# A two-layer graph kernel: the order of the first layer's pairs of chunks, and how far the last chunk's chain is spread among them

## Chip, cores and metric

The kernel runs on one core of a Trainium2 chip. The metric is the device time of one execution in microseconds (us), as a median of several runs.

## What is computed

`adj` is a 4096 x 4096 matrix with mostly zeros, `x` has 4096 rows of 128 numbers. First a graph layer in hyperbolic form adds `adj @ v` (with norms, tanh and atanh around two small products) to `x`. Then two attention layers run, each

```
x_norm = x / clip(norm(x), 1e-12)
scores = beta * (x_norm @ x_norm.T)
scores = where(a > 0, scores, -1e9)
x      = leaky(softmax(scores) @ x)
```

on `h = max(layernorm(x), 0)`, and the result is added to `x`. The scores are symmetric: the block of rows A against rows B is the transpose of rows B against rows A. The mask `a` is not symmetric.

## The kernel before

The 4096 rows are NC = 8 chunks of 512. The first stage (to about 282 us) multiplies `adj` by the features, chunk by chunk (`aggregate`), and behind each chunk comes a long chain of small instructions on VectorE and ScalarE that makes the rows of that chunk: lengths, tanh, logarithms, norms, layernorm, and at the end the normalised rows, which TensorE turns into columns `xt`. The chain of the last chunk, 7, is not over when TensorE is, so it is spread over the attention's first steps: `last_chunk(pause)` on ScalarE and VectorE calls `pause(i)` twelve times (PAUSES), and each call, by `between(i)`, is `slot(i + 1)`, one step of the attention.

The attention (`pairs`) works on pairs of chunks (a, b) with b >= a, row by row: a = 0 with b = 0 to 7, then a = 1 with b = 1 to 7, and so on. Each pair is two **halves** (lists at L292 to L308), numbered n from 0 to 143, 72 for each layer. The 16 halves with a = b are diagonal. For a half:

- TensorE makes the scores of 256 columns b against 512 rows a (`pair_scores`, L649).
- ScalarE raises them (`raise_scores`, L1078, one exponential of 128x1024 from PSUM) and makes the high 16 bits (`high_halves`, L1088). VectorE makes the low ones (`low_halves`, L1742).
- VectorE masks them with a tile of `adj` (`own_mask`, L1750), and TensorE adds them times `src` to the sums of row a (`own_sum`, L703 to L707), in the PSUM tile `own_ps`, which gathers a whole row.
- If a < b, TensorE also transposes them (`turns`, L635), VectorE masks the transposed block (`mirrored_mask`, L1760), and TensorE makes the sums for chunk b from it (`mirrored_sum`, L676 to L680) in `mir_ps`. These are added once per pair to `mirror_sums` in SBUF, by `flush` on VectorE (L1769); in row 0 they are the first, so ScalarE copies them (`first_flush`, L1096).

The order is written out by hand as steps n, and each engine has its own program of slots. TensorE in step n: scores of half n, mirrored sum and own sum of half n - 3, column sums if due, transposed columns if due, turns of half n - 1 (L737 to L756). ScalarE in slot n: columns that leave, then a row's first total (row a = 0) or a first flush, exponential n, high halves n, then averages, squares and normalised rows of rows that ended 4, 6 and 9 steps before (L1141). VectorE in slot n: flush of half n - 4, mirrored mask n - 2, a row's total, low halves n - 1, own mask n - 2, then columns, parts of the column sums, leaky (5 steps behind a row's end), the two parts of the scale (7 and 8 steps behind) (L1856). Semaphores join them; every engine works through its list in order.

`turned_at` gives the steps in which rows are turned into columns: chunk 7 of layer 0 at step 12 (LAST_CHUNK_AT), since scores 14 are the first that read it; chunk a of layer 1 ten or eleven steps behind the end of row a. `rows_summed` makes the column sums of `src`, chunk by chunk, in steps 4 to 8, 14 and 15 (SUMS_AT_OF); ScalarE takes them out in slot 16 and VectorE splits them in three parts, which TensorE adds, times a tiny number, to each row's own sum (L714). A row's own sum ends with its last half, is added to `mirror_sums` by `row_total` on VectorE (L1778), for row 0 only copied by ScalarE (`first_total`, L1102); the next row's first own sum waits for that by `total_made` (L694). SyncE loads the tiles of `adj` into six places in the order of the pairs; a load waits for the mask that used the tile six before it.

Of the kernel before, what the change touches and what calls it, by code (L numbers as in the profile page):

```python
# [26 lines left out]
def build(nc, x, adj, adj_t, embed, layer, embed_bias, layer_bias, beta1, beta2, out):  # L27
# [8 lines left out]
    CB = CH // P  # L36
# [30 lines left out]
    with ctx:  # L67
# [224 lines left out]
        Half = namedtuple("Half", "la a b h n off pair row own_tile mir_tile")  # L292
        Row = namedtuple("Row", "la a first last")
        half, rows_of, tile_of = [], [], []
        off_count = [0]
        for la in range(2):
            for a in range(NC):
                rows_of.append(Row(la, a, len(half), len(half) + 2 * (NC - a) - 1))
                for b in range(a, NC):
                    own_tile = len(tile_of)  # L300
                    tile_of.append((b, a, len(half) + 1, None))
                    if b > a:
                        tile_of.append((a, b, len(half) + 1, off_count[0] + 1))
                    for h in range(2):
                        off = off_count[0] if b > a else None
                        off_count[0] += b > a
                        half.append(Half(la, a, b, h, len(half), off, off // 2 if b > a else None, la * NC + a,
                                         own_tile, own_tile + 1))  # L308
# [5 lines left out]
        LAST_CHUNK_AT = 12  # L314
        turned_at = {LAST_CHUNK_AT: (0, NC - 1), **{rows_of[a].last + (11 if a == 5 else 10): (1, a) for a in range(NC)}}
        columns_before = {n: sum(m < n for m in turned_at) for n in turned_at}
        SUMS_AT = 2 * NC - 1
        SUMS_AT_OF = {4: (0, 1), 5: (2,), 6: (3,), 7: (4,), 8: (5,), 14: (6,), SUMS_AT: (7,)}

# [13 lines left out]
        PAUSES = 12  # L333
        ASKS_CHUNK = 6
# [96 lines left out]
        def _(pe):  # L431
# [208 lines left out]
            def pair_scores(x):  # L640

                wait(pe, raised, x.n)
                if x.a == 0 and x.h == 0:
                    pe.wait_ge(xt_lo[x.la], x.b + 1)
# [42 lines left out]
            def own_sum(x):  # L687

                r = rows_of[x.row]
# [3 lines left out]
                if x.n == r.first and x.row != LAST_ROW:  # L693
                    wait(pe, total_made, x.row)  # L694
                own_ps = own_of(x.row)
                if x.n % LAYER == SUMS_AT - 2:
                    pe.wait_ge(sums_copied, x.la + 1)
                w = halves(values[x.n % VR])
                for u in range(HB):
                    for ib in range(CB):  # L700
                        col, q = ds(u * CH + ib * P, P), x.b * CB + x.h * HB + u
                        opens = x.n == r.first and u == 0 and ib % 2 == 0
# [8 lines left out]
                if x.n == r.last:  # L711
# [16 lines left out]
            def columns_turned(n):  # L728
                la, c = turned_at[n]
                rows = rows_n[c % 2] if la else t3  # L730
                pe.wait_ge(xn_ready[la], c + 1)
# [5 lines left out]
            def pairs():  # L737
                for n in range(NH + 4):
# [9 lines left out]
                    if n % LAYER in SUMS_AT_OF and n < NH:  # L748
                        for c in SUMS_AT_OF[n % LAYER]:
                            rows_summed(n // LAYER, c)  # L750
# [20 lines left out]
        def _(act):  # L771
# [319 lines left out]
            def first_flush(x):  # L1091
# [3 lines left out]
                wait(act, total_made, x.la * NC)  # L1095
# [3 lines left out]
            def first_total(i):  # L1099
                act.wait_ge(row_summed, i + 1)  # L1100
# [11 lines left out]
            def row_squares(i):  # L1112
# [6 lines left out]
                nc.scalar.activation(src[1][:, ds(i * CB, CB), F:2 * F], rows_x[i % 2], ACT.Copy, scale=FS)\  # L1119
# [9 lines left out]
            def columns_leave(n):  # L1129
                la, c = turned_at[n]  # L1130
                act.wait_ge(xt_done[la], c + 1)
                if la:
                    wait(act, xt_lo[1], c)
# [7 lines left out]
            def slot(n):  # L1141
                if n % LAYER == SUMS_AT + 1:
                    la = n // LAYER
                    act.wait_ge(sums_done[la], 1)
                    if la:
                        act.wait_ge(row_summed, NC)
# [8 lines left out]
                if i is not None and rows_of[i].a == 0:  # L1155
# [5 lines left out]
                if i is not None and first:  # L1161
# [12 lines left out]
            def between(i):  # L1174

                slot(i + 1)

            def pairs():
                last_chunk(between)
                for n in range(PAUSES + 1, NH + 4):  # L1180
# [12 lines left out]
        def _(dve):  # L1193
# [570 lines left out]
            def flush(x):  # L1764
# [3 lines left out]
                kept = mirror_sums[:, ds(x.b * CB, CB), :].rearrange("p (k b) w -> p k (b w)", k=2)  # L1768
                V.tensor_tensor(kept, kept, mir_ps, ALU.add).then_inc(flushed, 1)  # L1769

            def row_total(i):
# [3 lines left out]
                if r.a:  # L1775
                    dve.wait_ge(row_summed, i + 1)
                    dve.wait_ge(flushed, half[r.first].la * NP + r.a * NC - r.a * (r.a + 1) // 2)
                    V.tensor_tensor(both, last_own_ps if i == LAST_ROW else own_ps, mirror_sums[:, ds(r.a * CB, CB), :]  # L1778
                                    .rearrange("p (k b) w -> p k (b w)", k=2), ALU.add).then_inc(total_made, 1)
                dve.wait_ge(total_made, i + 1)  # L1780
# [51 lines left out]
            def low_rows(i):  # L1832
                q = ds(i * CB, CB)
# [4 lines left out]
            def columns_low(n):  # L1838
                la, c = turned_at[n]
                dve.wait_ge(xt_hi[la], c + 1)  # L1840
# [15 lines left out]
            def slot(n):  # L1856
                x = at(n - 4)
                if x and x.off is not None and x.h == 1 and x.a:
# [5 lines left out]
                if i is not None and rows_of[i].a:  # L1864
# [3 lines left out]
                if i is not None and rows_of[i].a == 0:  # L1868
# [5 lines left out]
                if n % LAYER == SUMS_AT + 1:  # L1874
# [11 lines left out]
            def between(i):  # L1886

                slot(i + 1)

            def pairs():  # L1890
                last_chunk(between)
                for n in range(PAUSES + 1, NH + 1):
# [33 lines left out]
```

## Time and profile before

| | |
|---|---|
| median of 3 runs | 963.98 us (963.15 to 964.41) |
| profiled execution | 963.64 us |
| its span | 962.0 us |
| TensorE busy | 926.9 us, 96% |
| VectorE busy | 792.5 us, 82% |
| ScalarE busy | 538.0 us, 56% |
| granted TensorE clock | 0.997 of full speed |

Busy shares are means over the whole span; the attention begins with scores 0 at 281.7 us. The rows further down show single instructions: for the timelines, start, duration, engine, line, operation, output and inputs, and in brackets the idle time of the engine ahead of it and who ended it.

### The profile page before, as it was taken

What the parts mean: (1) busy time and instruction counts of PE and PEld (TensorE: products, weight loads), DVE (VectorE), ACT (ScalarE), POOL (GpSimd) and SP (SyncE); (2) the same over time, 40 slices, a digit from 0 to 9 for tenths busy, and PEclk for the clock granted to TensorE, in tenths of its full rate; (3) what the DMA queues carried; (4) which work ended last, traced back from release to release, by engine and by line L of the source; (5) the groups of instructions that cost most, each with busy time, mean ns of one, the idle gap of its engine ahead of it and who ended that gap; (6) DMA issues with size and microseconds to landing.
All of it is one profiled execution on the core that took longest, in us unless ns stands there. A gap on an engine that the chain in (4) does not pass through costs nothing.

```text
span 962.0 us, 22931 instructions
## 1 busy us (share of the span) xinstructions
PE 926.9 (96%) x9016; PEld 692.1 (72%) x9016; DVE 792.5 (82%) x1980; ACT 538.0 (56%) x867; POOL 7.2 (1%) x20
## 2 busy tenths in 40 slices
PE   7799999999997999999999999999999999999996
PEld 6644444444445878888888888778888888888886
DVE  7874778777789887978989898998788787888888
ACT  7802222232337766657656667796575565656564
POOL 0000000000000000000000000000000000000000
PEclk9999999999999999999999999999999999999998
DMA  8368888888851555455655545545455555565631
GB/s 298 154 222 289 283 298 293 279 286 283 293 180 57 232 196 210 186 202 198 249 195 212 220 180 216 210 160 201 177 219 219 232 206 201 220 228 194 259 144 37
DMA packets 30419, 207.26 MB, mean 215 GB/s; under 512 B 3632, under 2 KB 4784, under 8 KB 5744
## 3 DMA queue, kind: packets, MB, share of 16 engines
q1 hardware_dynamic: 28752, 203.70, 58.5%
q8 instruction: 71, 1.16, 0.5%
q0 software_dynamic: 560, 1.84, 0.5%
q10 hardware_dynamic: 1008, 0.33, 0.1%
q14 instruction: 28, 0.23, 0.1%
HBM read 203.75 MB, written 2.10 MB: 214 GB/s over the span
## 4 chain that ended last, share of the span: by engine, by line
PE 86%; ACT 6%; DVE 5%; issue 2%; DMA 0%; DVEq 0%; ACTq 0%
PE acc_ps L496 23%; PE s_ps L649 18%; PE s_ps L635 10%; PE acc_ps L707 6%; PE acc_ps L703 6%; PE acc_ps L705 6%; PE acc_ps L680 5%; PE acc_ps L676 5%; PE acc_ps L678 5%; ACT work L1078 1%; ACT set L800 1%; DVE work L1742 1%; PE s_ps L477 1%; ACT xt L822 1%; DVE work L1750 1%
## 5 line engine op out<-in xcount | busy, mean ns | idle before, releaser
L1078 ACT ACTIVATE work<-s_ps,beta_bias,beta_scale 128x1024 f32<-128x1024 f32 x144 | 173.5, 1205 | 212.2 <-PE s_ps L649 212.2
L496 PE MATMUL acc_ps<-ring,set 128*128 128x512 f32 x512 | 222.1, 592 | 1.6 <-DVE set L1348 1.6
L1760 DVE SCALAR_TENSOR_TENSOR h_all<-ring,s_ps 128x1024 f32<-128x1024 f32 x112 | 136.6, 1220 | 65.3 <-PE s_ps L635 63.9
L496 PEld LDWEIGHTS acc_ps<-ring,set 128*128 128x128 f32 x512 | 96.2, 190 | 117.5 <-issue 115.6
L1742 DVE TENSOR_TENSOR work<-work 128x1024 f16<-128x1024 f32 x96 | 132.7, 1382 | 5.4 <-ACT work L1088 5.4
L1088 ACT ACTIVATE work<-work 128x1024 f16<-128x1024 f32 x96 | 131.5, 1370 | 3.0
L1750 DVE SCALAR_TENSOR_TENSOR work<-ring,work 128x1024 f32<-128x1024 f32 x96 | 116.9, 1218 | 0.0
L649 PE MATMUL s_ps<-xt 128*128 128x512 f16 x432 | 105.4, 379 | 4.1 <-ACT work L1078 3.3
L649 PE MATMUL s_ps<-set 128*128 128x512 f16 x432 | 105.0, 379 | 0.5 <-ACT work L1078 0.5
L703 PE MATMUL acc_ps<-src,work 128*128 128x129 f16 x576 | 102.5, 219 | 2.0 <-DVE work L1750 2.0
L707 PE MATMUL acc_ps<-src,work 128*128 128x129 f16 x576 | 102.8, 222 | 0.0
L705 PE MATMUL acc_ps<-src,work 128*128 128x128 f16 x576 | 102.5, 219 | 0.0
L703 PE MATMUL acc_ps<-set,work 128*128 128x129 f16 x560 | 99.6, 219 | 1.2 <-DVE accs L1778 1.2
L707 PE MATMUL acc_ps<-set,work 128*128 128x129 f16 x560 | 99.9, 222 | 0.0
L705 PE MATMUL acc_ps<-set,work 128*128 128x128 f16 x560 | 99.7, 219 | 0.0
L680 PE MATMUL acc_ps<-src,h_all 128*128 128x129 f16 x448 | 79.8, 222 | 0.0
L680 PE MATMUL acc_ps<-set,h_all 128*128 128x129 f16 x448 | 79.8, 222 | 0.0
L676 PE MATMUL acc_ps<-src,h_all 128*128 128x129 f16 x448 | 79.6, 219 | 0.2 <-ACT ring L1096 0.2
L678 PE MATMUL acc_ps<-set,h_all 128*128 128x128 f16 x448 | 79.6, 219 | 0.0
L678 PE MATMUL acc_ps<-src,h_all 128*128 128x128 f16 x448 | 79.6, 219 | 0.0
L676 PE MATMUL acc_ps<-set,h_all 128*128 128x129 f16 x448 | 79.6, 219 | 0.0
L635 PE MATMUL s_ps<-ident,work 128*128 128x128 f32 x560 | 73.7, 275 | 2.3 <-DVE work L1742 2.3
(279 smaller groups left out, 1737.9 us busy)
## 6 DMA issues: line engine op xcount, KB each, us to landing
ring<-in_adj_t SPq DMA_DIRECT2D x192, 1024.0 KB, 5.0
x_sb<-in_x SPq DMA_DIRECT2D x4, 512.0 KB, 7.2
out<-x_sb POOLq DMA_DIRECT2D x7, 256.0 KB, 2.7
out<-x_sb SPq DMA_DIRECT2D x1, 256.0 KB, 2.7
w<-in_layer ACTq DMA_DIRECT2D x2, 64.0 KB, 8.2
w<-in_embed ACTq DMA_DIRECT2D x1, 64.0 KB, 4.5
eb<-in_embed_bias ACTq DMA_DIRECT2D x1, 64.0 KB, 6.9
lb<-in_layer_bias ACTq DMA_DIRECT2D x1, 64.0 KB, 7.9
```

The costliest lines, as they stand in the source:

```text
L496: last = nc.tensor.matmul(agg, v_sb[:, jb, :], ring[:, k, b, :], start=jb == 0, stop=jb == NB - 1)
L635: ins = nc.tensor.transpose(turn_ps[:, ib, ts(u, P)], words[x.n % WR][:, ds(u * CH + ib * P, P)], ident[:, :])
L649: last = nc.tensor.matmul(score_ps[:, ts(u, CH)], xt[x.la][:, p, ds(x.b * CH + (x.h * HB + u) * P, P)], xt[x.la][:, q, ds(x.a * CH, CH)], ...
L676: nc.tensor.matmul(mir_ps[:, x.h, o], w[:, WORD_HI, col], src[x.la][:, q, F:AW], start=ib == 0, stop=False)
L678: nc.tensor.matmul(mir_ps[:, x.h, ds(u * PW, F)], w[:, WORD_HI, col], src[x.la][:, q, 0:F], start=False, stop=False)
L680: last = nc.tensor.matmul(mir_ps[:, x.h, o], w[:, WORD_LO, col], src[x.la][:, q, F:AW], start=False, stop=ib == CB - 1)
L703: nc.tensor.matmul(own_ps[:, ib // 2, ds(ib % 2 * PW, PW)], w[:, WORD_HI, col], src[x.la][:, q, F:AW], start=opens, stop=False, skip_group ...
L705: nc.tensor.matmul(own_ps[:, ib // 2, ds(ib % 2 * PW, F)], w[:, WORD_HI, col], src[x.la][:, q, 0:F], start=False, stop=False, skip_group_c ...
L707: last = nc.tensor.matmul(own_ps[:, ib // 2, ds(ib % 2 * PW, PW)], w[:, WORD_LO, col], src[x.la][:, q, F:AW], start=False, stop=False, ski ...
L1078: nc.scalar.activation(values[x.n % VR], score_ps, ACT.Exp, bias=beta_bias[:, x.la:x.la + 1], scale=beta_scale[:, x.la:x.la + 1]).then_inc ...
L1742: V.tensor_tensor(w[:, WORD_LO, :], values[x.n % VR], w[:, WORD_HI, :], ALU.subtract)\
L1760: V.scalar_tensor_tensor(turned[x.off % MR].rearrange("p (b j) -> p b j", b=CB), ring[:, x.mir_tile % AR, :, ds(x.h * HB * P, HB * P)], 0. ...
```

## The change

In layer 0 the pairs come in another order. Row 0 is b = 0 to 6 (halves 0 to 13). Then comes row 1, b = 1 to 7 (halves 14 to 27). Then the pair of chunks 0 and 7 as a segment of its own, with the roles exchanged: a = 7, b = 0 (halves 28 and 29), so that its own sum belongs to chunk 7 and its mirrored sum to chunk 0. Rows 2 to 7 and layer 1 follow as before.

Chunk 7's columns are first read by scores 26 in place of 14. They are turned at step 24 in place of 12, and each pause of the last chunk's chain is two slots in place of one (SLOTS_PER_PAUSE). The column sums of layer 0 move to steps 18 to 23 and 27.

The own sum of row 0 is copied by ScalarE in slot 17 to `mirror_sums` (`own_kept`). When the late pair is done, VectorE adds to it the mirrored sum out of `mir_ps` and has row 0's total, and adds the late pair's own sum to the sums kept for chunk 7 (`late_total`, slot 33). The products with the parts of the column sums come for row 0 in the late pair's mirrored sum. The first mirrored sum for chunk 7 is now that of pair (1, 7), which VectorE copies instead of adding. Row 1 is over at half 27, row 0 at half 29; the order of chunks in `xn_ready`, `xt_lo` and the totals is counted by the new order.

```diff
+        LATE = NC - 1
+        kept_seg = add_seg(0, 0, range(LATE), None, 0)
+        seg = add_seg(0, 1, range(1, NC), 0, 1)
+        rows_of.append(Row(0, 1, seg.first, seg.last))
+        late_seg = add_seg(0, LATE, (0,), None, 2)
+        rows_of.append(Row(0, 0, kept_seg.first, late_seg.last))
+        LATE_ROW = 1
...
-        LAST_CHUNK_AT = 12
+        LAST_CHUNK_AT = 24
...
-        SUMS_AT_OF = {4: (0, 1), 5: (2,), 6: (3,), 7: (4,), 8: (5,), 14: (6,), SUMS_AT: (7,)}
+        SUMS_AT_LA = (rows_of[0].last, LAYER + 2 * NC - 1)
+        SUMS_AT_OF = {SUMS_AT_LA[0] - 11 + i: c for i, c in {2: (0, 1), 3: (2,), 4: (3,), 5: (4,), 6: (5,), 7: (6,),
+                                                             11: (7,)}.items()}
...
+        SLOTS_PER_PAUSE = 2
...
                         last = nc.tensor.matmul(mir_ps[:, x.h, o], w[:, WORD_LO, col], src[x.la][:, q, F:AW],
-                                                start=False, stop=ib == CB - 1)
+                                                start=False, stop=ib == CB - 1 and x.pair != late_pair)
+                    if x.pair == late_pair:
+                        last = nc.tensor.matmul(mir_ps[:, x.h, o], tiny[:, :], sums_parts, start=False, stop=True)
...
-                if x.n == r.first and x.row != LAST_ROW:
-                    wait(pe, total_made, x.row)
+                if x.n == seg.first and seg.row != LAST_ROW:
+                    wait(pe, total_made, seg.opens_after)
...
+            def own_kept():
+
+                act.wait_ge(own_added, kept_seg.last + 1)
+                nc.scalar.activation(mirror_sums[:, 0:CB, :].rearrange("p (k b) w -> p k (b w)", k=2), own_ps, ACT.Copy)\
+                    .then_inc(total_made, 1)
...
-                if i is not None and rows_of[i].a == 0:
+                own_leaves = n - 4 == kept_seg.last or (i is not None and i == NC)
+                if n - 4 == kept_seg.last:
+                    own_kept()
+                elif i == NC:
                     first_total(i)
...
-                slot(i + 1)
+                for n in range(SLOTS_PER_PAUSE * i + 1, SLOTS_PER_PAUSE * (i + 1) + 1):
+                    slot(n)
...
+                if x.la == 0 and (x.a, x.b) == (1, NC - 1):
+                    V.tensor_copy(kept, mir_ps).then_inc(flushed, 1)
+                    return
+                if x.la == 0 and x.a > 1 and x.b == NC - 1:
+                    dve.wait_ge(total_made, late_seg.opens_after + 1)
                 V.tensor_tensor(kept, kept, mir_ps, ALU.add).then_inc(flushed, 1)
+
+            def late_total():
+
+                late = mirror_sums[:, ds(LATE * CB, CB), :].rearrange("p (k b) w -> p k (b w)", k=2)
+                both, kept = (t.rearrange("p (k b) w -> p k (b w)", k=2) for t in (sums_in, mirror_sums[:, 0:CB, :]))
+                dve.wait_ge(mir_added, half[late_seg.last].off + 1)
+                dve.wait_ge(total_made, 2)
+                dve.wait_ge(flushed, late_pair)
+                V.tensor_tensor(both, kept, mir_ps, ALU.add).then_inc(flushed, 1)
+                dve.wait_ge(own_added, late_seg.last + 1)
+                V.tensor_tensor(late, late, own_ps, ALU.add).then_inc(total_made, 1)
+                dve.wait_ge(flushed, late_pair + 1)
+                V.reciprocal(fin[:, LATE_ROW % 2, 0, :], sums_in[:, :, F]).then_inc(inverse_made, 1)
...
-                if x and x.off is not None and x.h == 1 and x.a:
+                if n - 4 == late_seg.last:
+                    late_total()
+                elif x and x.off is not None and x.h == 1 and x.a:
                     flush(x)
```

The two changed lines of `between` stand alike on ScalarE and VectorE.

## Rows read from the trace of the kernel before

**Rows 1.** The page's share of the chain that ended last, by engine.
```profile
PE 86%; ACT 6%; DVE 5%; issue 2%; DMA 0%; DVEq 0%; ACTq 0%
```

**Rows 2.** Chain of waits, 290 to 480: start us, us, what.
```profile
315.26 1.09 PE s_ps L635 x8
...
396.20 1.29 PE s_ps L649 x6
400.25 0.88 PE s_ps L635 x8
```

**Rows 3.** Timeline of ScalarE, 360 to 412: start us, us, engine line operation [idle before <-releaser].
```profile
361.81 1.21 ACT L1078 ACTIVATE work<-s_ps,beta_bias,beta_scale 128x1024 f32<-128x1024 f32 x1 [2.34 <-PE s_ps L649]
...
367.18 1.21 ACT L1078 ACTIVATE work<-s_ps,beta_bias,beta_scale 128x1024 f32<-128x1024 f32 x1 [1.55 <-PE s_ps L649]
...
390.16 0.29 ACT L1116 ACTIVATE t<-t 128x128 f32<-128x128 f32 x1
...
391.32 0.62 ACT L1119 ACTIVATE set<-t 128x512 f16<-128x512 f32 x1
392.61 1.21 ACT L1078 ACTIVATE work<-s_ps,beta_bias,beta_scale 128x1024 f32<-128x1024 f32 x1 [0.67 <-PE s_ps L649]
```

**Rows 4.** Timeline of ScalarE, 276 to 366.
```profile
301.27 1.21 ACT L1078 ACTIVATE work<-s_ps,beta_bias,beta_scale 128x1024 f32<-128x1024 f32 x1 [3.61 <-PE s_ps L649]
...
306.47 1.21 ACT L1078 ACTIVATE work<-s_ps,beta_bias,beta_scale 128x1024 f32<-128x1024 f32 x1 [2.60 <-PE s_ps L649]
...
309.14 1.28 ACT L786 ACT_TABLE_LOAD   x1
...
325.69 0.28 ACT L910 ACTIVATE t<-t 128x128 f32<-128x128 f32 x1
...
329.10 1.21 ACT L1078 ACTIVATE work<-s_ps,beta_bias,beta_scale 128x1024 f32<-128x1024 f32 x1
```

**Rows 5.** Timeline of VectorE, 378 to 418.
```profile
391.31 1.22 DVE L1760 SCALAR_TENSOR_TENSOR h_all<-ring,s_ps 128x1024 f32<-128x1024 f32 x1 [0.93 <-PE s_ps L635]
392.45 1.38 DVE L1742 TENSOR_TENSOR work<-work 128x1024 f16<-128x1024 f32 x1
...
394.85 0.16 DVE L1820 TENSOR_SCALAR fin<-fin 128x4 f32<-128x4 f32 x1
...
396.04 0.69 DVE L1769 TENSOR_TENSOR ring<-ring,acc_ps 128x516 f32<-128x516 f32 x1
...
400.20 0.15 DVE L1814 TENSOR_TENSOR fin<-fin 128x4 f32<-128x4 f32 x1
...
402.04 1.22 DVE L1760 SCALAR_TENSOR_TENSOR h_all<-ring,s_ps 128x1024 f32<-128x1024 f32 x1
```

**Rows 6.** Timeline of VectorE, 280 to 350.
```profile
296.08 0.17 DVE L1473 COPY small<-small 128x4 f32<-128x4 f32 x1
...
297.50 1.29 DVE L1742 TENSOR_TENSOR h_all<-work,h_all 128x1024 f16<-128x1024 f32 x1
...
310.77 0.16 DVE L1247 TENSOR_TENSOR small<-small 128x4 f32<-128x4 f32 x1 [0.35 <-ACT small L786]
...
312.76 1.22 DVE L1760 SCALAR_TENSOR_TENSOR h_all<-ring,s_ps 128x1024 f32<-128x1024 f32 x1
...
321.75 1.14 DVE L1478 SCALAR_TENSOR_TENSOR t<-t,small,x_sb 128x128 f32<-128x128 f32 x4
...
324.10 1.22 DVE L1760 SCALAR_TENSOR_TENSOR h_all<-ring,s_ps 128x1024 f32<-128x1024 f32 x1
...
334.16 0.17 DVE L1488 TENSOR_SCALAR small<-small 128x4 f32<-128x4 f32 x1 [2.76 <-ACT t L925]
...
335.45 1.22 DVE L1760 SCALAR_TENSOR_TENSOR h_all<-ring,s_ps 128x1024 f32<-128x1024 f32 x1
```

**Rows 7.** Timeline of ScalarE, 600 to 660: marks 73 and 76.
```profile
625.08 1.21 ACT L1078 ACTIVATE work<-s_ps,beta_bias,beta_scale 128x1024 f32<-128x1024 f32 x1 [1.58 <-PE s_ps L649]
...
637.60 1.20 ACT L1078 ACTIVATE work<-s_ps,beta_bias,beta_scale 128x1024 f32<-128x1024 f32 x1
```

More of the change, by code:

```diff
@@ L290, in __call__ @@
                 self.eng.wait_ge(self.s, self.base + self.n)
-        Half = namedtuple("Half", "la a b h n off pair row own_tile mir_tile")
+        Half = namedtuple("Half", "la a b h n off pair seg own_tile mir_tile")
+        Seg = namedtuple("Seg", "first last row opens_after")
         Row = namedtuple("Row", "la a first last")
-        half, rows_of, tile_of = [], [], []
+        half, segs, rows_of, tile_of = [], [], [], []
         off_count = [0]
[L296 to L308, printed above, removed]
@@ new lines, in add_seg @@
+        def add_seg(la, a, bs, row, opens_after):
+            first = len(half)
+            for b in bs:
+                own_tile = len(tile_of)
+                tile_of.append((b, a, len(half) + 1, None))
+                if b != a:
+                    tile_of.append((a, b, len(half) + 1, off_count[0] + 1))
+                for h in range(2):
+                    off = off_count[0] if b != a else None
+                    off_count[0] += b != a
+                    half.append(Half(la, a, b, h, len(half), off, off // 2 if b != a else None, len(segs),
+                                     own_tile, own_tile + 1))
+            segs.append(Seg(first, len(half) - 1, row, opens_after))
+            return segs[-1]
@@ new lines, in build @@
+        LATE = NC - 1
[5 more added lines that the diff above has]
+        LATE_ROW = 1
+        for a in range(2, NC):
+            seg = add_seg(0, a, range(a, NC), a, a + 1)
+            rows_of.append(Row(0, a, seg.first, seg.last))
+        for a in range(NC):
+            seg = add_seg(1, a, range(a, NC), NC + a, NC + 1 + a)
+            rows_of.append(Row(1, a, seg.first, seg.last))
@@ L313, in build, with flushes_before, rows_summed_to, totals_to @@
         row_ending = {r.last: i for i, r in enumerate(rows_of)}
-        LAST_CHUNK_AT = 12
-        turned_at = {LAST_CHUNK_AT: (0, NC - 1), **{rows_of[a].last + (11 if a == 5 else 10): (1, a) for a in range(NC)}}
-        columns_before = {n: sum(m < n for m in turned_at) for n in turned_at}
-        SUMS_AT = 2 * NC - 1
-        SUMS_AT_OF = {4: (0, 1), 5: (2,), 6: (3,), 7: (4,), 8: (5,), 14: (6,), SUMS_AT: (7,)}
+        late_pair = half[late_seg.first].pair
+        def flushes_before(r):
+            return max([x.pair + 1 for x in half if x.off is not None and x.la == r.la and x.b == r.a], default=0)
+        def rows_summed_to(i):
+            return i + 1 - (i >= LATE_ROW)
+        def totals_to(i):
+            return i + 2
+        LAST_CHUNK_AT = 24
+        order_of = {(r.la, r.a): i for i, r in enumerate(rows_of)}
+        turned_at = {LAST_CHUNK_AT: (0, NC - 1), **{r.last + (11 if r.a == 5 else 10): (1, r.a) for r in rows_of[:NC]}}
+        columns_before = {n: sum(m < n for m in turned_at) for n in turned_at}
+        def turn_of(la, c):
+            return order_of[0, c] if la else c
+        SUMS_AT_LA = (rows_of[0].last, LAYER + 2 * NC - 1)
+        SUMS_AT_OF = {SUMS_AT_LA[0] - 11 + i: c for i, c in {2: (0, 1), 3: (2,), 4: (3,), 5: (4,), 6: (5,), 7: (6,),
+                                                             11: (7,)}.items()}
+        SUMS_AT_OF.update({LAYER + i: c for i, c in {4: (0, 1), 5: (2,), 6: (3,), 7: (4,), 8: (5,), 14: (6,),
+                                                     2 * NC - 1: (7,)}.items()})
         def tile_wait(eng, q):
@@ L710, in own_sum @@
                 last.then_inc(own_added, 1)
-                if x.n == r.last:
+                if x.n == seg.last and seg.row is not None:
                     pe.wait_ge(sums_split, 4 * x.la + 4)
@@ L1160, in slot @@
                     raise_scores(at(n))
-                if i is not None and first:
+                if own_leaves and first:
                     first_flush(x)
@@ L1863, in slot @@
                 i = row_ending.get(n - 4)
-                if i is not None and rows_of[i].a:
+                if i is not None and i not in (LATE_ROW, NC):
                     row_total(i)
@@ L1867, in slot @@
                     low_halves(at(n - 1))
-                if i is not None and rows_of[i].a == 0:
+                if i == NC:
                     row_total(i)
@@ L1886, in between @@
             def between(i):
-                slot(i + 1)
+                for n in range(SLOTS_PER_PAUSE * i + 1, SLOTS_PER_PAUSE * (i + 1) + 1):
+                    slot(n)
             def pairs():
                 last_chunk(between)
-                for n in range(PAUSES + 1, NH + 1):
+                for n in range(SLOTS_PER_PAUSE * PAUSES + 1, NH + 1):
                     slot(n)
```

52 lines of the change are left out of this document (27 added, 25 removed).

## Prediction

> **What bounds the kernel now.** I read the chain that ended last first: TensorE is 86% of it [rows 1], so what counts is when TensorE stands still or gets more work. Then I laid the starts of the exponentials (L1078) in a row. The exponential of half n starts when TensorE has finished the scores of half n, so its start is a clock for step n; I call it mark n. A regular step (scores 1.29, mirrored and own sums 400.25 - (396.20 + 1.29) = 2.76, turns 0.88) takes 4.93 us on TensorE alone [rows 2], and the later steps of the trace keep to it. A step whose finished half is diagonal has no mirrored sum (3.55); one whose newest half is diagonal has no turns (4.05). One chunk's column sum (rows_summed) costs 0.44: mark 15 to mark 16 is 5.37 [rows 3]. A transposed column is half of the turns, 0.44.
>
> Now the start. Mark 4 is at 301.27 [rows 4] and mark 15 at 361.81 [rows 3]: 60.54 us. TensorE's own work there is 11 x 4.93 = 54.2, less 1.38 for step 4, plus seven chunks' column sums 3.1, plus one transposed column 0.44: 56.4. So TensorE loses **4.1 us** between these marks, because VectorE and ScalarE carry the last chunk's chain between the slots. This is all that a wider spread can win there.
>
> **How much a slot can carry.** In an undisturbed slot n VectorE begins the mirrored mask 1.30 before mark n (391.31 against mark 22 at 392.61), the low halves end 1.22 after it (392.45 + 1.38), the own mask ends 2.24 after it (394.85) [rows 3, 5]. TensorE wants the low halves at mark + 2.76. So a slot may begin up to 1.5 us late without harm, and a piece of chain behind a slot may last 2.9 us (1.39 idle + 1.5). No piece of pure VectorE work is longer (the longest, chunk_sum, is 2.35: 321.75 to 324.10 [rows 6]). What is too long are the places where VectorE waits for an answer of ScalarE: ScalarE gives it only behind its own slot, at mark + 2.48 and later (the squares of row 0 began at 390.16 [rows 3], mark 21 is 392.61 - 4.93 = 387.68). These places have the same length whether one slot or two precede them. I go through them with the new order; "late" is how much later than usual VectorE begins the next slot.
>
> *Start.* Tanh, column 6's split and chunk_product now stand behind slots 1 and 2. VectorE then no longer has the first part of chunk_norms between the split and low halves 2 (296.08 to 297.50 [rows 6]), but low halves 1 and own mask 0 ahead of chunk_product, and reaches low halves 2 at about 296.5 and not at 297.50. Turns of half 2 go out about 0.95 earlier: mark 4 at 300.3. **Gain 1.0.**
>
> *Behind slot 4: squares (L903).* Four squares with their sums take 391.32 - 390.16 = 1.16 [rows 3]. Mark 4 + 2.48 + 1.16 + handover 0.15: VectorE goes on at mark + 3.8, its piece takes 297.50 - 296.08 = 1.42 [rows 6], slot 5 begins at mark + 5.2, the low halves are there at mark + 7.7, TensorE wanted them at 3.55 + 2.76 = 6.3. **Stop 1.4**, in step 5. Before, it was not waited for here.
>
> *Behind slot 10: logarithms.* With the table load (309.14, 1.28 us) VectorE goes on 4.30 after the mark (310.77 - 306.47) and needs 1.99 more (312.76) [rows 4, 6]. Slot 11 begins at mark + 6.29, low halves at + 8.8, wanted at 4.93 + 2.76 = 7.7. **Stop 1.1**, in step 11. Before, this place stood in a step that held a column sum for cover, and cost little by itself.
> The Trainium skill (ScalarE: Activation LUTs, "What ACT_TABLE_LOAD costs") gives 1283 ns for the load, as the row here, and about 1380 ns of drain on top of it; the row does not show that drain: from the start of the load to VectorE's next instruction, with two logarithms between, are 1.63 us. By the page the stop would be up to 1.4 us longer.
>
> *Behind slot 16: variances (L910, L915), then own_kept.* This is a new wait. Row 0's kept part ends with half 13, and the first own sum of the next segment (half 14, step 17 of TensorE) waits for total_made 1, which own_kept gives at the head of ScalarE's slot 17. Ahead of it in ScalarE's queue stands chunk_variances. Variances and a copy of 128x516 took 329.10 - 325.69 = 3.41 [rows 4]. own_kept is over at mark 16 + 2.48 + 3.41 + 0.05 = 5.9; TensorE is there at 4.05, since step 16 has no turns. Behind the waiting own sum are the turns of half 16 and scores 18. **Stop 1.9**, in step 17.
>
> *Behind slot 18: relu and squares.* VectorE waits here already now: it goes on at 334.16, idle 2.76, which is mark 9 (329.10) + 5.06, and begins the next slot at 335.45, mark + 6.35 [rows 4, 6]. In the new order step 18 has no mirrored sum and the column sums of two chunks (0.9): 4.45. Wanted: 4.45 + 2.76 + 0.45 (the next chunk's column sum) = 7.65; low halves at mark + 8.8. **Stop 1.15**, in step 19.
>
> *After each stop* TensorE is slow for a moment: the turns take 1.09 in place of 0.88 (315.26) [rows 2]. I add 0.2 for each of the four: 0.8.
>
> *Everything else in the chain* fits under the 2.9 us: product_scalars after slot 12, chunk_sum after 14, scales after 20, rows after 22, column 7 at 24. I cost these at nothing; their cover is the 1.39 us of VectorE per slot, and without it each would cost its length. Moved column sums (steps 18 to 23 and 27) keep their number: nothing. The four small products with the sums' parts leave row 0's own sum and come back in the late pair's mirrored sums: nothing. SyncE's tile loads follow the new order of the tiles, each still waits for the mask six tiles back: nothing. GpSimd's memset of layer 1's ones (L409) waits for the last chunk's rows and so goes out some 50 us later; layer 1 reads it 200 us after that: nothing. The copy that takes the place of the flush of pair (1, 7) reads the same 128x516 from PSUM as the add: at most the add's 0.69 [rows 5], at least nothing, and under VectorE's idle time either way.
>
> So the chain's stretch: -1.0 - 4.1 + 1.4 + 1.1 + 1.9 + 1.15 + 0.8 = **+1.2 us**.
>
> **The two row ends.** Row 1 (half 27) and row 0 (half 29) now end two steps apart. Steps 31 to 34 are short (4.05, 4.05, 3.55, 3.55), and into steps 33 to 37 fall two sets of averages, leaky, squares, scales. From the rows: squares with the copy 1.7 on ScalarE (390.16, 391.32 + 0.52), averages about as much as the four squares, 1.2, scale part one 1.19 on VectorE (394.85 to 396.04), part two with low rows 1.84 (400.20 to 402.04) [rows 3, 5], late_total two reads of 128x516 (0.69 each, 396.04) where a flush was one. ScalarE in slot 33 has averages and squares, 2.9: exponential 34 starts 1.8 late and scores 35 wait for it: stop 0.85. VectorE in slots 34 to 36 carries leaky, both parts for row 1, one for row 0; the flush of half 33 comes 0.6 after TensorE wants the bank: stop 0.6, in step 37. With a slow restart 1.6 in all; the two row ends of before lose about 0.3. **+1.3**. The nearest row of before is the end of layer 0, where rows 6 and 7 also end two apart: mark 73 (625.08) to mark 76 (637.60) is 12.5 us [rows 7] for work of 2.68 + 2.91 + 3.55 = 9.1, with four diagonal halves close together, so 3.4 at the worst; 0 is the other bound, if the 2.34 us per slot in which ScalarE is idle (mark 15 [rows 3]) swallow it. I take 1.3, nearer the middle, since here only steps 33 and 34 are that short.
>
> Layers and rows behind step 45 are as before. **Sum: +2.5 us.** The profiled execution took 963.64, 0.34 under the median 963.98. From it 966.1, beside the median **966.5**.
>
> **Rivals.**
> A, *the chain is hidden* (faster). If ScalarE's answers come before VectorE needs them, or the 2.9 us stretch to what the stops need, only the row ends are left: -1.0 - 4.1 + 1.3 = -3.8, **960.2**. For it: pieces of pure VectorE work all fit. Against it: the 2.76 us wait is in the trace and moves along. Chance 0.15.
> B, *stops replace stops* (no change). One or two of my stops, the new own_kept wait or the row ends first, are smaller: -1.9 to +1.9, centre 964.4. For it: each stop is a difference of some 8 us sums. Chance 0.33.
> C, *ScalarE bunches more* (slower still). The row ends cost the 3.4 of layer 0's end, or each load on ScalarE holds it for another load's time (1.28): +3.7 to +5.5, near **968**. Chance 0.08 and 0.02.
> The drain that the Trainium skill states for a table load would belong to this last one.
> D, *the change does not do what it says*: column 7 would still hold scores 26. Against it: rows are ready behind slot 22, at mark 22 + 5.4, while the transposes come at mark 24 + 2.8. Under 0.02, held in B.
> My forecast has 0.42 (its own range 965.9 to 967.6).
>
> **Numbers.** 0.2% is 1.9 us, about what a measurement of this kernel can tell from no change. Slower: 0.42 + 0.10 = 0.52. Within: 0.33. Faster: 0.15. The range from 961.8 to 968.8 leaves out most of A and the end of C.
>
> **What would show it.** Right: mark 4 near 300.3, marks 5 to 6 at 6.5 us, marks 10 to 12 together at 11.2, mark 17 to 18 at 5.4 to 5.5 with TensorE's own sum waiting for a copy of ScalarE, mark 19 to 20 at 6.8, VectorE idle 2.8 before the first instruction of chunk_deviations; marks 33 to 35 at 7.9, mark 37 to 38 at 6.0. From mark 45 on both kernels have the same steps. Wrong: steps 5, 11, 17, 19 at their own work (4.93, 4.93, 3.55, 5.4), which is A; or row ends without a stop, which leaves +1.2 (B).

## The result and the profile after

The changed kernel takes 968.16 us (967.16 to 969.98, 5 runs) beside 963.16 us (962.91 to 964.41, 5 runs) of the kernel before: ratio 1.0046, with a 95% interval of 1.0033 to 1.0058. By the ratio it is slower by 4.4 us (the two medians lie 5.0 apart). Forecast was +2.5, and 966.5 us counted from the median 963.98 of before. The profiled execution took 968.27 us, its span is 966.6.

The page of the changed kernel, its first part and the share of the chain that ended last [rows 1]:

```profile
PE 931.4 (96%) x9016; PEld 695.0 (72%) x9016; DVE 793.7 (82%) x1982; ACT 537.6 (56%) x866; POOL 7.2 (1%) x20
...
PE 86%; ACT 6%; DVE 5%; issue 2%; DMA 0%; DVEq 0%; ACTq 0%
```

The number of matmuls and the shares are the same, so the page's summary does not show where 4.4 us went. The marks do (mark n is the start of the exponential of half n, now L1119; "step n" with a time is the distance from mark n to mark n + 1). I took the starts from ScalarE's timelines of both kernels and of a second profile of each:

| from mark to mark | before | before, again | changed | changed, again | difference | forecast |
|---|---|---|---|---|---|---|
| 0 to 4 | 18.12 | 18.19 | 18.27 | 18.65 | +0.1 to +0.5 | -1.0 |
| 4 to 30 | 131.19 | 131.22 | 132.90 | 132.85 | +1.7 | +1.6 |
| 30 to 45 | 68.64 | 68.64 | 70.88 | 70.95 | +2.3 | +2.0 |
| 45 to 143 | 444.67 | 444.66 | 444.71 | 444.67 | 0.0 | 0 |

(The split of the forecast at mark 30 was made after the result: stops and slow restarts 6.35, less the 4.1 removed, is +2.25 from mark 4 to 30, and 0.67 us of work, a transposed column and four small products of row 0, has moved from there behind mark 30, where it adds to the 1.3 of the row ends.) The stops came as worked out. What failed is the start.

The changed kernel's marks 4, 5 and, further on, 16, 17 and 18, timeline of ScalarE (the kernel before: [rows 3, 4]); L951 is the first of the variances, L1149 is own_kept:

```profile
301.72 1.21 ACT L1119 ACTIVATE work<-s_ps,beta_bias,beta_scale 128x1024 f32<-128x1024 f32 x1 [2.38 <-PE s_ps L688]
...
305.43 1.21 ACT L1119 ACTIVATE work<-s_ps,beta_bias,beta_scale 128x1024 f32<-128x1024 f32 x1
...
361.48 1.21 ACT L1119 ACTIVATE work<-s_ps,beta_bias,beta_scale 128x1024 f32<-128x1024 f32 x1 [1.44 <-PE s_ps L688]
...
363.95 0.28 ACT L951 ACTIVATE t<-t 128x128 f32<-128x128 f32 x1
...
366.79 0.58 ACT L1149 ACTIVATE ring<-acc_ps 128x516 f32<-128x516 f32 x1
367.27 1.19 ACT L1119 ACTIVATE work<-s_ps,beta_bias,beta_scale 128x1024 f32<-128x1024 f32 x1
...
371.26 1.20 ACT L1119 ACTIVATE work<-s_ps,beta_bias,beta_scale 128x1024 f32<-128x1024 f32 x1 [1.07 <-PE s_ps L688]
```

The variances run from 363.95 to 366.79, own_kept at once behind them, with no idle time ahead of either: ScalarE's queue is full just where TensorE needs the copy. Who waited, in the changed kernel between 301 and 400 us (engine and line, what it waited for, us in total, times, longest):

```profile
PE s_ps L672 <- DVE work L1793: 3.4, 3, 1.2
DVE small L1539 <- ACT t L966: 2.8, 1, 2.8
...
PE acc_ps L744 <- ACT ring L1149: 2.0, 1, 2.0
DVE small L1298 <- ACT small L827: 1.9, 1, 1.9
DVE small L1524 <- ACT t L944: 1.4, 1, 1.4
```

There are three waits of VectorE for ScalarE's answers (relu 2.8, logarithms 1.9, squares 1.4), three waits of TensorE for low halves (together 3.4), and one for own_kept (2.0). In the kernel before VectorE did not wait for the squares at all and 0.35 us for the logarithms; the wait for relu is as long as before to the hundredth [rows 6], with two slots ahead of it instead of one:

```profile
376.33 0.17 DVE L1539 TENSOR_SCALAR small<-small 128x4 f32<-128x4 f32 x1 [2.76 <-ACT t L966]
...
377.61 1.22 DVE L1811 SCALAR_TENSOR_TENSOR h_all<-ring,s_ps 128x1024 f32<-128x1024 f32 x1
```

The two row ends, timeline of ScalarE, marks 33, 34, 35, then 37, 38:

```profile
448.10 1.21 ACT L1119 ACTIVATE work<-s_ps,beta_bias,beta_scale 128x1024 f32<-128x1024 f32 x1 [1.55 <-PE s_ps L688]
...
453.43 1.18 ACT L1119 ACTIVATE work<-s_ps,beta_bias,beta_scale 128x1024 f32<-128x1024 f32 x1
...
456.17 1.21 ACT L1119 ACTIVATE work<-s_ps,beta_bias,beta_scale 128x1024 f32<-128x1024 f32 x1 [0.18 <-PE s_ps L688]
...
466.02 1.20 ACT L1119 ACTIVATE work<-s_ps,beta_bias,beta_scale 128x1024 f32<-128x1024 f32 x1 [1.20 <-PE s_ps L688]
...
472.14 1.21 ACT L1119 ACTIVATE work<-s_ps,beta_bias,beta_scale 128x1024 f32<-128x1024 f32 x1 [0.91 <-PE s_ps L688]
```

Exponential 34 has no idle time ahead of it: ScalarE is late. Marks 33 to 35 are 8.07 apart for 7.1 of work, and step 37 takes 6.12 for 5.37 of work.

**The start.** TensorE's timeline of the changed kernel, scores 1, 2, 3, turns 2, scores 4:

```profile
284.71 1.47 PE L688 MATMUL s_ps<-xt 128*128 128x512 f16 x6
...
289.92 2.74 PE L688 MATMUL s_ps<-xt 128*128 128x512 f16 x6 [1.62 <-ACT work L1119]
...
293.96 2.74 PE L688 MATMUL s_ps<-xt 128*128 128x512 f16 x6 [1.30 <-ACT work L1119]
...
299.30 1.09 PE L672 MATMUL s_ps<-ident,h_all 128*128 128x128 f32 x8
300.23 1.46 PE L688 MATMUL s_ps<-xt 128*128 128x512 f16 x6
```

The same six matmuls take 1.47 us and then twice 2.74. The view by stretches of the changed kernel gives the reason (columns: stretch, us, busy time and number for TensorE, its loads, VectorE, ScalarE and GpSimd, then granted clock, DMA share, GB/s):

```profile
283.00:289.50 6.50, 3.84 (x24) 2.36 (x22) 4.99 (x29) 5.92 (x16) 0.00 (x0) 0.96 0.00 0
289.50:299.50 10.00, 8.28 (x38) 4.34 (x39) 8.03 (x17) 7.39 (x8) 0.00 (x0) 0.51 0.01 2
```

and the same of the kernel before:

```profile
283.00:289.50 6.50, 3.53 (x23) 2.17 (x21) 5.02 (x28) 6.22 (x16) 0.00 (x0) 1.00 0.00 0
289.50:299.50 10.00, 5.13 (x42) 3.04 (x43) 9.31 (x24) 8.07 (x16) 0.00 (x0) 1.00 0.01 2
```

TensorE was at 1.2 GHz there (granted clock 0.51), after a stretch in which it had been busy 3.84 of 6.5 us. But both kernels do the same up to 289.6 us, so this profile alone doesn't tell whether the change has a part in it.

### The profile page after: what moved, and what is told of

Its sections match the earlier page's. It is cut to its first block, busy times and chain, and to the rows that moved or that the text cites. A ratio compares the mean times of both kernels' runs of the same rounds, so it can differ in the third digit from the quotient of the medians.

```text
span 966.6 us, 22930 instructions
## 1 busy us (share of the span) xinstructions
PE 931.4 (96%) x9016; PEld 695.0 (72%) x9016; DVE 793.7 (82%) x1982; ACT 537.6 (56%) x866; POOL 7.2 (1%) x20
## 4 chain that ended last, share of the span: by engine, by line
PE 86%; ACT 6%; DVE 5%; issue 2%; DMA 0%; DVEq 0%; ACTq 0%
PE acc_ps L533 23%; PE s_ps L688 18%; PE s_ps L672 10%; PE acc_ps L748 6%; PE acc_ps L744 6%; PE acc_ps L746 6%; PE acc_ps L719 5%; PE acc_ps L715 5%; PE acc_ps L717 5%; ACT work L1119 1%; DVE work L1793 1%; ACT set L841 1%; PE s_ps L514 1%; ACT xt L863 1%; DVE work L1801 1%
## 5 line engine op out<-in xcount | busy, mean ns | idle before, releaser
L1119 ACT ACTIVATE work<-s_ps,beta_bias,beta_scale 128x1024 f32<-128x1024 f32 x144 | 173.4, 1204 | 216.5 <-PE s_ps L688 216.5
L688 PE MATMUL s_ps<-xt 128*128 128x512 f16 x432 | 107.9, 386 | 4.4 <-ACT work L1119 3.6
L744 PE MATMUL acc_ps<-src,work 128*128 128x129 f16 x576 | 103.6, 220 | 2.0 <-ACT ring L1149 2.0
L748 PE MATMUL acc_ps<-src,work 128*128 128x129 f16 x576 | 103.9, 224 | 0.0
```

The lines of the kernel that those rows point to most:

```text
L688: last = nc.tensor.matmul(score_ps[:, ts(u, CH)], xt[x.la][:, p, ds(x.b * CH + (x.h * HB + u) * P, P)], xt[x.la][:, q, ds(x.a * CH, CH)], ...
L744: nc.tensor.matmul(own_ps[:, ib // 2, ds(ib % 2 * PW, PW)], w[:, WORD_HI, col], src[x.la][:, q, F:AW], start=opens, stop=False, skip_group ...
L1119: nc.scalar.activation(values[x.n % VR], score_ps, ACT.Exp, bias=beta_bias[:, x.la:x.la + 1], scale=beta_scale[:, x.la:x.la + 1]).then_inc ...
```

## Experiments

There are three comparisons, each with its own runs of the kernel before, and each ratio is to these: 963.56 us (21 runs) for both kernels again and with ten idle products, 963.91 (26) for the variances, the squares and logarithms, all four answers and row 0's work, 963.45 (21) for the idle products that fit and for everything together. Across comparisons only ratios are compared.

### Both kernels again

No edit.

> The kernel before, unchanged, for the clocks of its executions. In the profile of the changed kernel TensorE stood at half clock from 289.1 to 299.4 us, and scores 2 and 3 took 2.74 us each in place of 1.47. Up to 289.6 both kernels do the same. Theory P (the drop is a matter of phase, not of the change): some executions of this kernel have it too, the mean clock lies between 0.985 and 0.997 and the times spread by 1 to 2 us. Theory Q (the change brings it): all executions at 0.995 to 0.997, scores 2 and 3 at 1.47.

> The changed kernel, unchanged. Theory P: some executions without the drop, at about 966.5 us, and others with it at 967.5 to 968.5. Theory Q: the drop at the same place again, scores 2 and 3 at 2.74 us, mark 4 near 301.7. In both the marks from 5 on have the same distances as in the first profile: 6.4, 4.9 ... and from mark 45 on those of the kernel before.

Before: 963.66 us, ratio 1.0 (0.9991 to 1.0009). Changed: 967.86 us, 1.0053 (1.0040 to 1.0067). In the profile of the kernel before, scores 2 took 2.74 us this time; mark 0 to mark 4 was 18.19, so the half clock cost it nothing (0.07 us):

```profile
289.81 2.74 PE L649 MATMUL s_ps<-xt 128*128 128x512 f16 x6 [1.62 <-ACT work L1078]
...
299.11 1.09 PE L635 MATMUL s_ps<-ident,h_all 128*128 128x128 f32 x8 [1.18 <-DVE h_all L1742]
```

In the changed kernel it came later, at the turns of half 2 and scores 4:

```profile
297.49 1.97 PE L672 MATMUL s_ps<-ident,h_all 128*128 128x128 f32 x8 [2.48 <-DVE h_all L1793]
299.25 2.29 PE L688 MATMUL s_ps<-xt 128*128 128x512 f16 x6
```

Turns 2 went out 14.57 us behind mark 0, as forecast (low halves 2 at 296.5 would put them at 14.7 behind 283.15), and then TensorE lost 1.7 us on turns and scores. In the kernel before they went out 15.77 behind mark 0 (mark 0 is 283.34), and TensorE stood idle ahead of them for 1.18 us, not 2.48.

Theory Q, that the kernel before never has the drop, fell. P stands only in part. The drop at scores 2 comes without the change. The one at turns 2 was in five profiles, all of the changed order and all with 2.5 us of idle time ahead of turns 2, and in neither profile of the kernel before, so the change may well have a part in that one; no run tests it. The mean clock of single executions can't decide it (0.985 to 0.998 in the eleven runs of the kernel before), since profiles have half clock in the kernel's first 45 us as well (0.66 to 0.70 in stretches of 5 us of this one).

### Idle products in the gaps

Ten products (twenty instructions in the trace) whose result nobody reads, in each of three gaps; the edit, the same for both kernels, with WARM_STEPS = 10:

```diff
                     if n == 1:
+                        idle_products(WARM_STEPS)
                         before_last_columns()
+                    if n in (1, 2):
+                        idle_products(WARM_STEPS)
```

> The changed kernel with three lots of ten idle products (128x128, each 0.11 us) for TensorE in the gaps of steps 1 and 2. If the half clock at 289 to 299 costs what I think, it is gone: scores 2 and 3 take 1.47, mark 4 comes at 300.4 to 300.7 and the time falls by 1.0 to 1.4 us beside the changed kernel. If the clock has no part, or the gaps are not what brings it down, time within 0.5 us of the changed kernel.

> The kernel before with the same idle products. Theory P: as fast as the fastest executions of the kernel before, less spread (962.9 to 963.3). Theory Q: no change, 963.2 plus or minus 0.5. If the products themselves delay the scores (they fill only gaps of 1.5 us), up to 0.3 slower.

Changed: 967.53 us, 1.0039 (1.0025 to 1.0053). Before: 963.91, 1.0001 (0.9992 to 1.0010). Both profiles have full clock in the start, but ten products took 2.4 us, not 1.1, longer than the gaps; scores 2 came 1.0 us late, and mark 0 to 4 in the changed kernel was 17.98, not 17.2. That is inconclusive for the cost, so I cut the products to fit (the edit against the kernels without idle products):

```diff
+                    if n == 3:
+                        idle_products(8)
                     if done:
                         own_sum(done)
...
                     if n == 1:
+                        idle_products(5)
                         before_last_columns()
+                    if n in (1, 2):
+                        idle_products(5)
```

> The changed kernel with idle products that fit TensorE's gaps: five (1.2 us) in each of the three gaps of steps 1 and 2, eight ahead of own sum 0 (the ten of before took 2.4 us and pushed scores 2 by 1.2). Theory (the start gains 1.0 us only if TensorE is at full clock between 289 and 301): no half clock there, mark 4 at mark 0 + 17.2 to 17.4 in place of 18.27 and 18.65, and 1.0 to 1.4 us off the time. Rival (something else holds the start): mark 0 to mark 4 at 18 or more with the clock full.

> The kernel before with the same idle products. Its scores 2 and 3 have slack: VectorE's chain orders the start, so a half clock there cost it nothing (mark 0 to 4 was 18.12 at full clock and 18.19 with 3.4 us at half). Theory: mark 0 to 4 stays at 18.1 to 18.2, time within 0.4 us. Rival (the clock costs both kernels the same): 0.5 us or more less.

TensorE's timeline of the changed kernel with them (L473 are the idle products):

```profile
288.33 1.28 PE L473 MATMUL acc_ps<-ident 128*128 128x128 f32 x10
290.13 1.47 PE L688 MATMUL s_ps<-xt 128*128 128x512 f16 x6 [0.52 <-ACT work L1124]
291.44 1.28 PE L473 MATMUL acc_ps<-ident 128*128 128x128 f32 x10
292.90 1.47 PE L688 MATMUL s_ps<-xt 128*128 128x512 f16 x6 [0.19 <-ACT work L1124]
```

Mark 0 to 4 is 17.02 at full clock: the start's gain of 1.0 us is there once the clock holds (the forecast's marks gave 17.15). In the kernel before it is 18.11, no gain: there VectorE's chain orders the start, and turns 2 go out 15.7 us behind mark 0 at full clock as at half. The time of the changed kernel did not follow: 967.70 us, 1.0042 (1.0029 to 1.0056), where 1.0 to 1.4 less was expected. Its profile has half clock at another stop, that of step 17:

```profile
366.50:370.50 4.00, 3.94 (x33) 3.90 (x34) 0.00 (x0) 2.75 (x3) 0.00 (x0) 0.58 0.81 266
```

Marks 16 to 18 took 11.41 us there, in place of 9.78. But the profiled execution was the slowest of the five (968.68). The other four took 967.19 to 967.79 at a higher mean clock (0.995, not 0.992), and 968.68 less 1.63 is 967.05, so this stop explains the profiled execution and not the median. For the changed kernel the gain of the start is thus shown in the marks of one profile and not in the time; why the time did not follow is open. Before: 963.77 us, 1.0004 (0.9995 to 1.0013).

Over all profiles of this study, the granted clock between 289 and 302 us was 0.61 to 0.88 in eight of the nine without idle products (only the first profile of the kernel before had 1.00), and 1.00 in all five with them.

### Variances one slot earlier

ScalarE calls them behind slot 15 and not 16 (`slots(a, b)` calls slots a to b; `pause(i)` was slots 2i + 1 and 2i + 2):

```diff
-                for i in (6, 7):
-                    pause(i)
+                slots(13, 15)
                 chunk_variances()
-                pause(8)
+                slots(16, 18)
```

> The changed kernel; ScalarE makes the variances of the last chunk behind slot 15 in place of slot 16, so that own_kept no longer stands behind them. Theory (ScalarE's queue makes the stop in step 17): TensorE's 2.0 us of waiting for that copy is gone, marks 16 to 18 are 7.6 to 7.8 us apart in place of 9.78, and the time falls by about 2.0 us beside the changed kernel. Rival (the place is one where all engines are full, so the stop comes back behind it): marks 16 to 18 shorter, marks 18 to 20 longer by the same, time within 0.5.

966.23 us, 1.0026 (1.0016 to 1.0036): 1.9 to 2.6 us less than the changed kernel, by its ratios of 1.0046 and 1.0053. Timeline of ScalarE, marks 16 to 18 with own_kept (L1151):

```profile
362.61 1.18 ACT L1121 ACTIVATE work<-s_ps,beta_bias,beta_scale 128x1024 f32<-128x1024 f32 x1
...
365.04 0.57 ACT L1151 ACTIVATE ring<-acc_ps 128x516 f32<-128x516 f32 x1
365.51 1.19 ACT L1121 ACTIVATE work<-s_ps,beta_bias,beta_scale 128x1024 f32<-128x1024 f32 x1
...
369.50 1.20 ACT L1121 ACTIVATE work<-s_ps,beta_bias,beta_scale 128x1024 f32<-128x1024 f32 x1 [1.06 <-PE s_ps L688]
```

Marks 16 to 18 are 6.89 apart in place of 9.78, but exponential 16 starts 1.3 late behind the variances; marks 15 to 18, which hold both, went from 13.81 to 12.22. So 1.6 us are won in the marks (expected were 2.0), and steps 18 and 19 are unchanged (5.45, 5.80): nothing came back behind it. ScalarE's queue made this stop.

### Squares and logarithms one slot earlier

```diff
-                pause(1)
+                slots(3, 3)
                 chunk_squares()
-                for i in (2, 3, 4):
-                    pause(i)
+                slots(4, 9)
                 log_terms(sm(4, CB), sm(5, CB), sm(6, CB))
```

> The changed kernel; ScalarE makes the squares behind slot 3 in place of 4 and the logarithms behind slot 9 in place of 10. Theory (VectorE waits for an answer that comes too late in ScalarE's slot): VectorE no longer idles there (1.43 and 1.9 us now), step 5 falls from 6.37 to 4.93 to 5.2, marks 10 to 12 from 11.17 to 9.9, together 2.7 us less. Rival (the length of VectorE's own piece makes the stops): steps unchanged, time within 0.5.

966.34 us, 1.0020 (1.0011 to 1.0030), in ten runs from 964.52 to 967.22. Timeline of ScalarE, marks 5 and 6, then the two table loads and mark 10 behind them:

```profile
305.87 1.21 ACT L1121 ACTIVATE work<-s_ps,beta_bias,beta_scale 128x1024 f32<-128x1024 f32 x1 [1.06 <-PE s_ps L688]
...
310.80 1.21 ACT L1121 ACTIVATE work<-s_ps,beta_bias,beta_scale 128x1024 f32<-128x1024 f32 x1 [2.31 <-PE s_ps L688]
...
328.20 1.28 ACT L827 ACT_TABLE_LOAD   x1
...
329.81 1.28 ACT L1121 ACT_TABLE_LOAD   x1
331.11 1.21 ACT L1121 ACTIVATE work<-s_ps,beta_bias,beta_scale 128x1024 f32<-128x1024 f32 x1
```

Step 5 is 4.93, no stop. Marks 10 to 12 are 9.22, but exponential 10 itself stands behind the two table loads, and marks 9 to 12 are 14.76, three steps of work. Both stops are gone, 2.8 us together in the marks. VectorE's piece is as long as it was, so it is the late answer and not the piece.

### All four answers early

Variances and the two above, and relu behind slot 17 in place of 18:

```diff
-                for i in (6, 7):
-                    pause(i)
+                slots(13, 15)
                 chunk_variances()
-                pause(8)
+                slots(16, 17)
                 chunk_relu(c)
-                pause(9)
+                slots(18, 20)
```

> The changed kernel with all four answers of ScalarE one slot earlier: squares behind slot 3, logarithms behind 9, variances behind 15, relu behind 17. Theory: the first three stops go (4.8 us). The fourth, in step 19 (5.80 with 5.46 ahead of it), goes too, but the relu now makes exponential 18 some 2.6 us late, and scores 19 wait 0.7 for it: so 0.4 to 0.6 won there. In all 5.2 us less than the changed kernel, about 962.7. Rival as in the runs beside it: what goes in one step comes back in the next, 966 or more.

962.07 us, 0.9985 (0.9976 to 0.9995): faster than the kernel before, and by the ratios 6 us under the changed one, where 5.2 less was expected. Marks 4 to 20 went from 80.80 to 75.13 us, which is 5.7; the start of this profile was short too, 17.46 us from mark 0 to 4 (18.27 and 18.65 in the changed kernel's). Step 19 is 5.37, its own work; exponential 18 stands behind relu and is late, and marks 17 to 19 take 8.54, for 8.0 of work. No run gives the kernel before its answers one slot earlier, so how much of the lead over it is owed to the new order isn't shown.

### Row 0's work three slots later

`row_worked` is `row_ending` with half 29 counted as 32, and averages, leaky, squares, scales, normalised rows and columns go by it; row 0's total stays.

```diff
+        LATE_BY = 3
+        row_worked = {r.last + (LATE_BY if i == LATE_ROW else 0): i for i, r in enumerate(rows_of)}
...
+                i = row_worked.get(n - 4)
                 if i is not None and i != LAST_ROW:
                     row_averages(i)
-                i = row_ending.get(n - 6)
+                i = row_worked.get(n - 6)
```

> The changed kernel; the averages, leaky, squares, scales, normalised rows and columns of row 0 come three slots later (its total stays), so that the two row ends lie five steps apart. Theory (two sets of row work in slots 33 to 37 make the stops): marks 33 to 35 from 8.07 to 7.2, step 37 from 6.12 to 4.9 to 5.4, marks 30 to 45 from 70.9 to 69.4 or 69.6, time 1.3 to 1.5 us less. Rival (the stop comes from late_total and the short steps themselves): marks 33 to 35 stay at 8, time within 0.4.

Marks 33 to 35 fell from 8.07 to 7.25, step 37 from 6.12 to 5.35, marks 30 to 45 to 69.79 (1.1 less; expected were 1.3 to 1.5). The timeline of ScalarE at marks 33 to 35:

```profile
447.71 1.21 ACT L1121 ACTIVATE work<-s_ps,beta_bias,beta_scale 128x1024 f32<-128x1024 f32 x1 [1.55 <-PE s_ps L690]
...
451.87 1.18 ACT L1121 ACTIVATE work<-s_ps,beta_bias,beta_scale 128x1024 f32<-128x1024 f32 x1
...
454.96 1.21 ACT L1121 ACTIVATE work<-s_ps,beta_bias,beta_scale 128x1024 f32<-128x1024 f32 x1 [0.53 <-PE s_ps L690]
```

The time doesn't show it: 968.34 us in five runs from 966.33 to 968.88, 1.0043 (1.0029 to 1.0057). Its spread is wider than the effect. The marks are the evidence here, the time is inconclusive.

### Everything together

> The changed kernel with the four early answers and row 0's work three slots later. If the stops are separate, their gains add: 5.6 from mark 4 to mark 20 and 1.2 from mark 30 to 45, so marks 4 to 45 take 197.0, against 203.8 in the changed kernel and 199.85 before; time about 961, 3 us under the kernel before. If they share a cause, less than 6 together.

> The same with the idle products of the first run. Gains add with the start's: mark 4 at mark 0 + 17.2, marks 4 to 45 197.0, about 960, the fastest of all. If the products only heat a place that does not matter: as the run without them.

The four early answers and the later row: 961.07 us, 0.9981 (0.9971 to 0.9990); marks 4 to 45 took 197.06 us as the sum of the single gains said (changed 203.8, before 199.8). Its eleven runs lie between 960.32 and 963.22. In this profile the half clock began at turns 2 again (scores 4 took 2.77), and mark 0 to 4 was 18.44. With the idle products that fit the gaps: 959.49 us, 0.9959 (0.9945 to 0.9973), the fastest of all, 8.2 us under the changed kernel with the same idle products (967.70) and 4.0 under the kernel before. Its timeline of ScalarE, marks 0 and 4:

```profile
283.02 1.20 ACT L1128 ACTIVATE work<-s_ps,beta_bias,beta_scale 128x1024 f32<-128x1024 f32 x1 [0.70 <-PE s_ps L690]
...
300.05 1.20 ACT L1128 ACTIVATE work<-s_ps,beta_bias,beta_scale 128x1024 f32<-128x1024 f32 x1 [2.30 <-PE s_ps L690]
```

That is 17.03 us, and from mark 4 to 45 it is 196.96. Its five runs lie between 959.22 and 959.79, all under the eleven without the idle products: here the 1.4 us that the start gained in the marks is in the time too (1.6), and the spread is smaller.

## Why the prediction was right, and where it was off

- **Direction and mechanism: right.** Pieces of VectorE's own work fit in a slot; what doesn't is VectorE waiting for ScalarE. Two slots per pause took none of these waits away. The one for relu stayed at 2.76; the ones for squares and logarithms rose from nothing to 1.43 and from 0.35 to 1.90, since VectorE comes to them with less behind it; and own_kept is a new wait, of TensorE.
- **The removed 4.1 us**: confirmed. Steps 6 to 9 and 12 to 14 of the changed kernel are 4.93 each.
- **Stops, forecast against measured**: step 5, 6.5 against 6.37; marks 10 to 12, 11.2 against 11.17; marks 18 to 20, 11.25 against 11.26; marks 33 to 35, 7.9 against 8.07; step 37, 6.0 against 6.12. Marks 16 to 18 were 9.78, 0.3 over the 9.5 of the forecast's marks and 0.1 over its sum with the slow restart. I had put all of that stop between marks 17 and 18; exponential 17 itself stands behind own_kept, so 5.79 lies ahead of mark 17 and 3.99 behind it. In the same way step 18 was 5.46 and not 4.45, and step 19 5.80 and not 6.8: exponential 19, without idle time ahead of it, stands behind relu and its squares. Where ScalarE is late a mark no longer shows when TensorE was done, and only the distance over two steps can be compared.
- **The table load**: the Trainium skill's drain (ScalarE: Activation LUTs, "What ACT_TABLE_LOAD costs"), which by the estimate from that page would have made marks 10 to 12 up to 1.4 us longer, doesn't show in them: 11.17 is the sum without it, and in the squares-and-logarithms kernel the second load is over at 331.09 and the exponential starts at 331.11.
- **The failed step is the start**, "Gain 1.0". Its mechanism was right, and 17.02 us is what it gives at full clock. But in the changed kernel's two profiles it came out as a loss of 0.1 to 0.5. I had not asked what lies on the path once VectorE's chain does not: scores 2 and 3, turns 2 and scores 4, in a stretch where TensorE is busy 3.4 to 4.0 of 6.5 us and fell to 1.2 GHz in eight of nine profiles. In the kernel before the same fall costs nothing (18.12 and 18.19). By the marks this is 1.1 to 1.5 us of the 1.9 us between the forecast difference and the measured one; the time alone doesn't show it, since the idle products brought the changed kernel's ratio down by 0.4 to 1.1 us, within its interval. Row ends add 0.3: 1.6 in place of 1.3. (One term of theirs was misread: the copy behind the squares takes 0.62 us in [rows 3], not 0.52.) The little that is left, and the spread of the changed kernel's runs (967.2 to 970.3 over both comparisons), could come from half clock at a stop in some executions, as in the one profile at step 17, but the runs behind the medians have no trace; that part is open.
- **Range and rivals**: 968.2 lies inside 961.8 to 968.8, but above the forecast's own 965.9 to 967.6. It is near C's centre (968), but for neither of C's reasons: the row ends cost 1.6, not 3.4, and no load held ScalarE longer. B needed one or two stops or the row ends smaller, and none was. A (960.2) needed the answers early, and with the answers early the kernel came to 962.1.

## What to carry to other kernels

When a chain is spread between the slots of a loop, sum up not the chain's instructions but the point within the slot at which each answer of the other engine can come; twice as many slots per pause help the pieces that are work and do nothing for those that wait (here the wait for relu stayed at 2.76 us). Ask for the answer one slot ahead of its use, on the engine that gives it, and keep it out of the slot in which that engine has to free an accumulator. A new order that brings two row ends together pays for both in the same slots; three slots of distance took 1.1 of the 1.6 us back.

## What the runs showed of the hardware

TensorE fell from 2.4 to 1.2 GHz in or near the start in eight of the nine profiles without idle products. In all nine it had been busy 3.4 to 4.0 of the 6.5 us from 283.0 on. In three the clock fell at scores 2 or just ahead of them, with idle gaps of up to 1.6 us before; in the other five, all of the changed order, it fell at turns 2, behind 2.5 us of idle time. At half clock the same six matmuls took 2.74 us in place of 1.47. Idle products in three gaps (2.4 us each in two profiles; 1.28 us each, and 1.95 in a fourth gap, in three) went with full clock from 289 to 302 us in all five profiles that had them, and cost the kernel before nothing that its time shows (1.0001 and 1.0004). They did not keep the clock up elsewhere: one of the five fell at step 17. Whether the fall costs anything depends on what waits: by the marks nothing in the kernel before, 0.4 to 1.7 us in the kernels of the changed order (17.46 to 18.67 from mark 0 to 4 beside 17.02), and 1.6 us where it hit the stop of step 17.

A switch of ScalarE's table cost the length of the load, 1.28 us, and no more, in the profile of the squares-and-logarithms kernel: the exponential began 0.02 us behind the second load, 331.11 against 331.09.
